# A fourth PSUM bank in the ring of the count products of a graph-network kernel

## The reference

```
msg = x[src] + edge_attr                       # one row of 128 per edge
agg = segment_sum(msg, dst)                    # per target node
h   = relu(agg @ W1 + b1) @ W2 + b2
h   = normalised over everything, then per feature, gelu
out = layernorm(x + (h + x))
```

## Time and profile before

| | |
|---|---|
| median of three runs | 868.77 us (866.02 to 869.89) |
| the profiled execution's own time | 871.19 us |
| its span, first to last instruction | 869.1 us |
| PE busy | 725.3 us, 83% |
| DVE busy | 680.7 us, 78% |
| ACT busy | 385.5 us, 44% |
| the 25 chunks | about 121 to 771 us of the span |

### The profile page before, as it was taken

One profiled execution on the slowest core, in us unless ns is written; L12 is line 12 of the kernel. 1 busy time (PEld: TensorE's weight loads), 2 busy tenths in 40 slices (PEclk: granted clock), 3 DMA queues, 4 the chain that ended last, 5 costly groups with the idle time before them and its releaser, 6 DMA issues.

```text
span 869.1 us, 25816 instructions
## 1 busy us (share of the span) xinstructions
PE 725.3 (83%) x9449; PEld 628.6 (72%) x9449; DVE 680.7 (78%) x1189; ACT 385.5 (44%) x841; POOL 84.7 (10%) x67
## 2 busy tenths in 40 slices
PE   3576679988999988999988899988899988889940
PEld 3464458877888877788877788877788877778730
DVE  5755768988888888888888898888898898814575
ACT  0110034466544466544456644456644456604454
POOL 1221001011011011101101101101101101000000
PEclk9987869999999999999999999999999999989985
DMA  6769993455333445433455433355433345213004
GB/s 161 258 203 354 359 324 109 148 154 152 113 107 103 140 154 154 115 115 109 123 154 154 127 107 112 116 154 154 130 107 108 116 153 154 78 42 114 0 1 148
DMA packets 88855, 123.45 MB, mean 142 GB/s; under 512 B 8479, under 2 KB 84348, under 8 KB 88635
## 3 DMA queue, kind: packets, MB, share of 16 engines
q1 hardware_dynamic: 78992, 112.83, 41.9%
q0 software_dynamic: 5616, 5.25, 2.2%
q10 hardware_dynamic: 4228, 5.12, 1.9%
HBM read 119.10 MB, written 4.03 MB: 142 GB/s over the span
## 4 chain that ended last, share of the span: by engine, by line
PE 66%; ACT 10%; issue 9%; DMA 7%; DVE 5%; ACTq 1%; DVEq 1%; SPq 0%
PE bank L693 34%; PE bank L672 12%; PE bank L622 11%; ACT counts L520 8%; DMA edges<-in_edge_attr_dram 6%; PE bank L740 3%; PE bank L636 3%; PE bank L750 2%; DMA agg<-in_dst_dram 1%; ACT sums L490 1%; PE bank L595 1%; DVE pool_m L826 1%; DVE pool_m L1189 1%; ACT pool_m L584 1%; PE bank L777 0%
## 5 line engine op out<-in xcount | busy, mean ns | idle before, releaser
L520 ACT CAST counts<-bank 128x490 fp32r<-128x490 f32 x625 | 319.6, 600 | 309.0 <-PE bank L672 304.9
L693 PE MATMUL bank<-counts,x_hi 128*128 128x250 f32 x1225 | 289.5, 281 | 29.6 <-ACT counts L520 29.6
L693 PE MATMUL bank<-counts,x_lo 128*128 128x250 f32 x1225 | 286.9, 279 | 0.0
L693 PEld LDWEIGHTS bank<-counts,x_hi 128*128 128x128 f32 x1225 | 231.6, 189 | 33.4 <-ACT counts L520 33.4
L977 DVE TENSOR_TENSOR pool_m<-listing,turned_lo 128x3328 bf16<-128x3328 bf16 x125 | 235.9, 1887 | 17.9 <-ACT turned_key L500 17.9
L672 PE MATMUL bank<-pool_m 128*128 128x98 bf16 x3125 | 210.6, 209 | 26.2 <-ACT counts L520 14.9
L693 PEld LDWEIGHTS bank<-counts,x_lo 128*128 128x128 f32 x1225 | 232.0, 189 | 0.0
L672 PEld LDWEIGHTS bank<-pool_m 128*128 128x128 bf16 x3125 | 158.8, 98 | 76.8 <-ACT counts L520 73.1
L977 DVE TENSOR_TENSOR pool_m<-listing,turned_key 128x2548 bf16<-128x2548 bf16 x125 | 184.9, 1479 | 0.0
L622 PE MATMUL bank<-edges,onehot 128*32 128x128 f32 x3228 | 129.6, 297 | 23.8 <-DMA edges<-in_edge_attr_dram 21.1
L622 PEld LDWEIGHTS bank<-edges,onehot 128*32 128x32 f32 x3228 | 90.5, 118 | 40.9 <-issue 22.1
(11 more groups left out here) (149 smaller groups left out, 410.5 us busy)
## 6 DMA issues: line engine op xcount, KB each, us to landing
edges<-in_edge_attr_dram SPq DMA_DIRECT2D x134, 768.0 KB, 5.9
out_dram<-pool_m SPq DMA_DIRECT2D x6, 512.0 KB
agg<-in_dst_dram SPq DMA_DIRECT2D x1, 768.0 KB
agg<-in_src_dram ACTq DMA_DIRECT2D x1, 768.0 KB
listed<-agg ACTq DMA_DIRECT2D x1, 768.0 KB
begins<-listed,tile_slot POOLq DMA_INDIRECT x27, 5.1
begins<-listed,row_slot POOLq DMA_INDIRECT x27, 3.4
w<-in_L_gnn_W_dram ACTq DMA_DIRECT2D x2, 128.0 KB, 2.2
```

Source lines behind the costliest of these rows:

```text
L520: nc.scalar.copy(counts[:, :, k * nodes:(k + 1) * nodes].rearrange("p q (i m) -> p q i m", m=PAIR), cps[k % RING][:, 0:nodes * NT].rearran ...
L693: last = nc.tensor.matmul(sps[:, 0:CHUNK], part[:, q, :], counts[:, q, :], start=(q == 0 and part is x_hi), stop=(q == NT - 1 and part is ...
```

## The change

`RING` becomes 4, and the idle bank 5 becomes the ring's fourth. PE may fill bank k as soon as bank k - 4 is copied. No instruction is added, removed or moved; each chunk has one wait on `banks_free` less (21 for 22), and the others ask for one copy less.

```diff
-RING = 3
+RING = 4
@@
-        cps = banks[0:RING]
+        cps = banks[0:3] + banks[5:6]
```

## The result

| | before | with four banks |
|---|---|---|
| median, us | 867.97 (4 runs, 866.02 to 869.89) | 856.83 (4 runs, 853.19 to 895.15) |
| ratio | | 0.9858, interval 0.981 to 0.9905 |
| the profiled execution's own time | 871.19 | 858.36 |
| its span | 869.1 | 856.4 |
| mean granted clock over the span | 0.957 | 0.928 |

The kernel is faster by 1.4%, 11.1 us by the medians of the table; 842.1 was predicted, with a range of 837 to 850.5, so the time lies above the range. The highest of the four, 895 us, had a mean granted clock of 0.826 for a reason that isn't known and is left out of the ratio; the median of the other three is 855.3.

A forecast was written before the change was run, and what follows sets the result against it. PE and ACT took turns on the chain, with DVE's round next to bound; 1.08 us per chunk, some 26.7 in all, off 871.2 gave 844.5, less 2.4 for that execution's offset: 842.1 us, range 837 to 850.5.

The forecast's parts named there:

- those gaps: ACT's lost time behind three bursts in the count stage: 0.38 + 0.54 + 0.38 = 1.30 us per chunk, nearly all to go.
- The wait for keys on DVE: DVE's 0.83 us wait before the start at 266.79; claimed to go because keys come 1.22 earlier.
- the 1.29 in front of L1045: DVE's gap before that add, 1.30 us in the prediction; claimed to be DVE's own work and to stay unchanged.
- The sum: Gain of 25.91 - 24.83 = 1.08 us per chunk, together some 26.7 us, giving 842.1 us.
- the step on the clock: PE's granted clock is 1.00 through the chunks; the trace shows no fall, so it adds nothing to the forecast.
- the slower rival: Changed PE pattern makes the clock fall once in each chunk, 76 us less 26.7: 918 us; chance 0.04.
- My own walk through the banks: Step-by-step timing of the count stage's banks up to bank 21; PE and ACT alone gain about 1.22 us per chunk.
- DVE sets the chunk: DVE's shortest round, 24.83 us, exceeds PE and ACT's 24.70, so PE waits for batch 4's marks before bank 20.
- DVE is already the bound: DVE's round can't shrink and PE only waits longer for marks: 868.8 us; chance 0.09.
- The weak gain: DVE keeps its small wait of 0.25, round 25.08, gain 20.8 us: 848.0 us; chance 0.12.
- The strong gain: DVE's slip costs nothing, gain 1.22 us per chunk, 30.5 us in all: 838.3 us; chance 0.12.
- The finding of no further gain from double-buffering in PSUM: A skill page's report on another kernel; by it the gain would be 0 and the time 868.8 us.

The follow-up runs named there:

- the filled pause: Four-bank kernel plus twelve matmuls with unread results in PE's pause in front of the products; median 841.45 us, ratio 0.9689.
- the moved burst: Four-bank kernel with the fourth burst moved from behind bank 20 to behind bank 24; median 838.37 us, ratio 0.9664.
- the split pause: Four-bank kernel in which banks 22 to 24 wait as in a ring of three; median 858.52 us, ratio 0.9891.

## Why the prediction was wrong

**What held.** The kernel before lost what the rows said behind three of its four bursts: those gaps are gone, the first one isn't, and the count stage is 1.19 shorter, against 1.22 reckoned. The chunk without a fall is 24.81 against 24.83. The wait for keys on DVE is gone, and the 1.29 in front of L1045 is still there, DVE's own as I had it. With the clock kept up, the kernel takes 841.45 us; 842.1 was predicted. The sum is right within a microsecond, but not every reason in it: that DVE's round gave the right number for the chunk is luck (see below).

**What failed: the step on the clock.** I had the clock's fall as the slower rival, with a chance of 0.04, and gave one reason against it: "PE's pauses get shorter in sum, not longer". In sum they did. But the ring moves PE's standing: what stood spread over the count stage, in short pieces between bank matmuls (73 us of waits of PE's weight loads before, 26.5 now), shrank, and PE stood 0.47 us longer at the one place where it stood longest already. My own walk through the banks had PE one copy further ahead and ended at bank 21; I didn't follow it to the end of the stage, and put the lengthened pause there at nothing. There the next wait is for the last copy, and who comes earlier to a wait whose end is set by another engine waits longer.

**The price and the count.** I priced a fall at 3.05, half of a 6.10 us stretch in the dense part; here one costs 1.57, since the stretches are shorter, some 3.4 us. I counted one per chunk or none; there were 11 in 25. 11 x 1.57 = 17 us of the 26.7 won, which leaves about 10; 11 were measured (and 26.6 with the filled pause). The rival was put as one that turns the sign (918 us), and so the case between, a clock that falls in some chunks and takes half of the gain, was in no sum and outside the range.

The Trainium skill, TensorE: Matmul & The Clock Gate, section A second HAM failure mode: psum-queue depth-cycling, says that small pauses of TensorE between groups while it cycles through PSUM banks can let the clock fall and rise again. The changed kernel's rows agree with it (0.57 in the stretch behind the pause), and the filled pause shows that here it is the standing in front of the products. I had set it aside because the trace before showed 1.00 throughout. That trace only said that the pauses of before made no fall.

**A smaller error, without effect on the number.** "DVE sets the chunk" is not so. PE and ACT's own loop is 24.82, not 24.70: the last copy takes 0.74 instead of 0.63, so the products start 0.79 behind its start instead of 0.68. That DVE's shortest round came out at 24.83 is a coincidence: with the moved burst it goes round in 24.69, and in the kernel with the filled pause the chunk stays at 24.81 when a load is taken out of DVE's round. PE did not wait for the marks of batch 4 in the changed kernel.

**The rivals.** *DVE is already the bound* is refuted: its round shrank by 1.1 as soon as the keys came earlier. *The weak gain* would need DVE's small wait in front of L880; in the changed kernel's chunk at 272.95 no wait stands there. *The strong gain* took PE and ACT's loop as 24.70, and that loop is 24.82. The finding of no further gain from double-buffering in PSUM (the Trainium skill, TensorE: Matmul & The Clock Gate, section HAM oscillation — how this bites in real kernels) does not carry over to this kernel: its chunk lost 1.1 us.

**What stays open.** What exactly must be exceeded isn't settled, neither as one pause nor as a sum: the kernel before has no fall with its pause of 1.18, the split pause falls with 1.18 and short pieces close to it, and the moved burst has none with 0.90 and 0.69. Why the falls come in every second chunk in one kernel and in others irregularly wasn't tested.

## What to carry to other kernels

A deeper buffer lets the producer finish earlier, and at a point where both engines meet it then stands longer; follow the walk to that point, not only to the gap that closes. Where PE stands there before a long stretch of matmuls, a granted clock of 1.00 in the profile is no reserve: put some of PE's own work (here a burst) into that pause. And a mechanism that comes in some rounds and not in others belongs into the range with half its price, not only into the rivals at its full one.

## What the runs showed of the hardware

- A stretch at half clock (some 3.4 us) that begins within half a us or so of the products' start costs 1.57 us on top of a stage of 11.67. It came in a part of the chunks (11 of 25) behind a pause of 1.65, in 14 of 25 behind 1.79 with three banks, and in 8 of 25 behind 1.18 with short pieces ahead of it; in the profiled chunks of the kernel before, with 1.18, it never came.
- ACT's copies start 0.46 us apart, but the last one takes 0.63 in the profile where ACT had waited for PE three copies earlier (264.16 in the earlier trace rows), and 0.74 behind a group of twelve without a visible gap. Since the copies start 0.46 apart all the same, only the last one's length is on the path.
- Two register loads in a row on DVE's sequencer cost nearly as much as two apart: 1.98 us of DVE's idle time per chunk against 2.09.
